# A modulation stage written anew: reversed rows from the input, the norm in the weights, the bias in PSUM

## The chip, the cores and the metric

The program runs on one core of one Trainium2 chip. The metric is the device time of one launch in microseconds (us). Engines are named as in the profile: PE (TensorE, with its weight loads as PEld), DVE (VectorE), ACT (ScalarE), POOL (GpSimd) and SP, which issues most transfers. A line such as L1242 is a line of the kernel before, if nothing else is said.

## The reference

The program computes a text/vision block and a quantised feed-forward over 4096 rows of 512 channels. Attention (not touched) leaves, for each row, a vector `u` of 384 numbers, and `c_t @ W_film_in` is computed as `u` times weights folded beforehand. What the change touches is the input modulation, which stands in front of a convolution along the rows:

```python
def _layernorm(x, axis=-1, eps=1e-05):
    m = jnp.mean(x, axis=axis, keepdims=True)
    v = jnp.var(x, axis=axis, keepdims=True)
    return (x - m) / jnp.sqrt(v + eps)
...
x = layernorm(x_text, g_norm_in, b_norm_in)      # x_text is itself _layernorm(x)
scale_in, shift_in = jnp.split(c_t @ W_film_in + b_film_in, 2, axis=-1)
x = x * (1.0 + mod_gate * scale_in) + mod_gate * shift_in
y = s4d(x, log_dt, A_re, A_im, C_re, C_im, D_skip)
```

## The kernel before

The program is a row of phases with a barrier between each two: `prepare`, `attention`, `modulate`, `s4d`, `feed_forward`, `bit_feed_forward`. Each engine has its own written-out instruction stream, in a fixed order, and waits on semaphores. Only `modulate` is changed (and the host's layout of one input).

`modulate` handles 32 tiles of 128 rows, with the two buffers of each name used in turn, tile n in buffer n % 2. `prepare` has left the normalised input in `scratch_xt` and the folded weights in `scratch_wf_in` (384 x 1024: 512 columns for the scale and 512 for the shift), `attention` has left `scratch_u` (4096 x 384). For each tile:

- SP loads `mod_xt` (L1187, when DVE has read that buffer, `xt_read`) and `mod_u` (L1189, when PE has turned it).
- PE turns `u` by three transposes into `mod_tp` (L1319). ACT rounds it into the high part of `mod_uT` (L1277), DVE subtracts for the low part (L1236).
- PE multiplies (L1329): high x high, high x low, low x high, three chunks each, 9 matmuls of 512 columns for the scale and 9 for the shift, into `mod_film`.
- DVE takes the mean and variance of `xt` (L1226, L1228), ACT the root (L1273), DVE the reciprocal (L1230) and the normalised tile `mod_xn` (L1232). POOL multiplies by the gain (L1201) and adds the offset (L1203).
- DVE adds the film bias to both halves (L1242, L1243), multiplies by `xn` (L1246) and adds the shift (L1249) into `mod_xm`.
- `s4d` wants the rows of each tile in reversed order. ACT rounds `xm` into a high part (L1284), POOL subtracts for the low part (L1207), PE multiplies both with a matrix of ones on the other diagonal (L1338, L1339) into `mod_rev`, and ACT copies that into `X` (L1290), where successive channels lie 32 numbers (128 bytes) apart.

Before the loop, the weights are loaded whole and split into high and low parts by DVE (L1254, L1256). In the loop, one turn of DVE is `normalise(n + 1)` then `film(n)`; one turn of PE is `turn_u(n + 2)`, `film(n + 1)`, `reverse(n)`; one turn of ACT is `root(n + 2)`, `copy_u(n + 2)`, `high_x(n)`, `copy_x(n)`.

Of the kernel before, what the change touches and what calls it, by code (L numbers as in the profile page):

```python
# [1145 lines left out]
def modulate(nc, sem, const, a, W, root_table, wf, fb, X, dram):  # L1146

# [3 lines left out]
    with scope:  # L1151
# [15 lines left out]
        rstd = sb("mod_rstd", [P, 1])
        tp = [ps(f"mod_tp{k}", [P, VC, P]) for k in range(2)]
        fp = [ps(f"mod_film{k}", [P, 2, BANK]) for k in range(2)]
        rp = [ps(f"mod_rev{k}", [P, BANK]) for k in range(2)]  # L1170
        x_by_channel = X[:].rearrange("p c d -> p (c d)").rearrange("p (d c) -> p d c", c=TILES)
        s = {n: sem("mod_" + n) for n in (
            "wf_loaded", "tables_in", "rows_in", "in0", "in1", "xt_read", "u_turned", "uT_ready", "film_done", "film_read", "std_wanted", "std_ready",
            "normed", "affine", "diag_made", "wf_split", "uT_high", "xm_ready", "xm_high", "xm_split", "reversed", "X_ready", "passed")}

        with nc.Block() as block:
            @block.sync
            def _(sp):
                sp.dma_start(wf[:], dram["wf_in"][:, :, :]).then_inc(s["wf_loaded"], 16)
                sp.dma_start(fb[:], dram["fb"][1, :].partition_broadcast(P)).then_inc(s["rows_in"], 16)  # L1180
                sp.dma_start(gain[:], a["g_norm_in"].partition_broadcast(P)).then_inc(s["rows_in"], 16)
                sp.dma_start(offset[:], a["b_norm_in"].partition_broadcast(P)).then_inc(s["rows_in"], 16)
                with sp.Fori(0, TILES // 2) as i:
                    for b in range(2):
                        n = 2 * i + b
                        sp.wait_ge(s["xt_read"], n + 1)
                        sp.dma_start(xt[:, b], dram["xt"][bass.ts(n, P), :]).then_inc(s[f"in{b}"], 16)  # L1187
                        sp.wait_ge(s["u_turned"], n + 1)
                        sp.dma_start(u[:, b], dram["u"][bass.ts(n, P), :]).then_inc(s[f"in{b}"], 16)  # L1189

            @block.gpsimd
            def _(pool):
                nc.gpsimd.memset(other_diag[:], 0.0)
                pool.drain()
                nc.gpsimd.affine_select(out=other_diag[:], in_=other_diag[:], compare_op=ALU.not_equal, fill=1.0,
                                        base=1 - P, pattern=[[1, P]], channel_multiplier=1).then_inc(s["diag_made"], 1)
                pool.wait_ge(s["rows_in"], 48)

                def affine(m, b):
                    pool.wait_ge(s["normed"], 2 * m + b + 1)  # L1200
                    nc.gpsimd.tensor_tensor(xn[:, b], xn[:, b], gain[:], ALU.mult)  # L1201
                    pool.drain()
                    nc.gpsimd.tensor_tensor(xn[:, b], xn[:, b], offset[:], ALU.add).then_inc(s["affine"], 1)  # L1203

                def low_x(m, b):
                    pool.wait_ge(s["xm_high"], 2 * m + b + 1)
                    nc.gpsimd.tensor_tensor(xm_parts[:, b, 1], xm[:, b], xm_parts[:, b, 0].bitcast(F32), ALU.subtract).then_inc(s["xm_split"], 1)  # L1207

                pool.sem_inc(s["xm_split"], 2)
                affine(0, 0)  # L1210
                with pool.Fori(0, TILES // 2 - 1) as i:
                    for b in range(2):
                        affine(*after(i, b))
                        low_x(i, b)
                affine(TILES // 2 - 1, 1)
                low_x(TILES // 2 - 1, 0)
                low_x(TILES // 2 - 1, 1)

            @block.vector
            def _(dve):  # L1220
                dve.sem_inc(s["xt_read"], 2)

                def normalise(m, b):
                    n = 2 * m + b
                    dve.wait_ge(s[f"in{b}"], 32 * (m + 1))
                    nc.vector.bn_stats(stats[:], xt[:, b, :])  # L1226
                    dve.drain()
                    nc.vector.bn_aggr(mv[:], stats[:]).then_inc(s["std_wanted"], 1)  # L1228
                    dve.wait_ge(s["std_ready"], n + 1)
                    nc.vector.reciprocal(rstd[:], rstd[:])  # L1230
                    dve.drain()
                    nc.vector.tensor_scalar(xn[:, b], xt[:, b], mv[:, 0:1], rstd[:, 0:1], ALU.subtract, ALU.mult).then_inc(s["normed"], 1)  # L1232
                    dve.drain()
                    dve.sem_inc(s["xt_read"], 1)
                    dve.wait_ge(s["uT_high"], n + 1)
                    nc.vector.tensor_tensor(uT[:, b, 1], tp[b][:], uT[:, b, 0].bitcast(F32), ALU.subtract).then_inc(s["uT_ready"], 1)  # L1236

                def film(m, b):
# [24 lines left out]
                normalise(TILES // 2 - 1, 1)
# [1658 lines left out]
```

## Time and profile before

| what | us |
|---|---|
| median of 3 runs | 4269.23 (4267.5 to 4271.36) |
| the profiled execution, its time | 4266.21 |
| the profiled execution, its span | 4264.4 |
| of that: modulation, from its first transfer's issue (1963.38) to the end of its last copy into X (2206.45 + 1.02) | 244.1 |

Over the span PE is busy 78%, DVE 76%, ACT 54% and POOL 33%, at a mean granted TensorE clock of 0.834. Phases stand behind one another with a barrier, so a phase's length goes whole into the time, and an engine's share over the span tells nothing of this phase. The views that follow are of the stretch from 1963 to 2208 us.

### The profile page before, as it was taken

To read this page: it belongs to the slowest core of one execution; us is meant where nothing else is said; L and a number is where in the kernel's file an instruction comes from. 1 tells how busy PE (TensorE), PEld (TensorE's weight loads), DVE (VectorE), ACT (ScalarE), POOL (GpSimd) and SP (SyncE) were. 2 spreads that over 40 slices of the span, in tenths; PEclk is the share of its full clock that TensorE was granted. 3 is DMA by queue.
4 is the path that set the end of the run, shared out by engine and by line. 5 is a ranking of instruction groups with operands and counts; after the bars stand their busy time and mean duration, and the time that the engine had idled before them with its cause. 6 is when DMAs were issued, how large, how long until landed. Compare 5 with 4: busy or idle time off the path is not lost. (4 is left out here: it accounts for less than half of the span.)

```text
span 4264.4 us, 55224 instructions
## 1 busy us (share of the span) xinstructions
PE 3337.1 (78%) x16624; PEld 2225.8 (52%) x16624; DVE 3241.3 (76%) x8831; ACT 2284.6 (54%) x3031; POOL 1425.2 (33%) x1265
## 2 busy tenths in 40 slices
PE   7665858888888888876757778568999999936776
PEld 3343535555555555544545555357777777712333
DVE  7699999999999999986889999334443434369996
ACT  4574858887778888882323333223332332337774
POOL 0022424444444444443551010023233323205664
PEclk9756767777777777778978998889999999968888
DMA  8600000000000000002212343444433333330111
GB/s 321 242 6 9 10 5 9 9 9 12 9 11 9 9 9 9 9 7 90 67 33 52 88 104 86 119 138 144 124 129 123 126 116 92 121 92 26 54 49 53
DMA packets 263808, 291.04 MB, mean 68 GB/s; under 512 B 55450, under 2 KB 177436, under 8 KB 262368
## 3 DMA queue, kind: packets, MB, share of 16 engines
q1 hardware_dynamic: 240504, 255.10, 19.6%
q10 hardware_dynamic: 19976, 17.80, 1.5%
q0 software_dynamic: 3040, 14.94, 0.9%
q8 instruction: 102, 1.67, 0.2%
q14 instruction: 186, 1.52, 0.1%
HBM read 219.34 MB, written 68.45 MB: 67 GB/s over the span
## 5 line engine op out<-in xcount | busy, mean ns | idle before, releaser
L1061 PE MATMUL score<-KT,q 64*128 64x512 f32 (+1 forms) x1792 | 669.9, 522 | 276.5 <-ACT S L918 159.8
L815 DVE MAX8 cand<-S 128x8 f32<-128x100 f32 (+1 forms) x4096 | 680.4, 245 | 69.9 <-ACT S L918 50.2
L1061 PEld LDWEIGHTS score<-KT,q 64*128 64x128 f32 x1792 | 439.6, 264 | 509.5 <-ACT S L918 219.6
L1089 PE MATMUL up<-ctx,attnT 128*128 128x384 f32 (+1 forms) x1664 | 614.1, 518 | 0.0
L918 ACT ACTIVATE S<-score 128x1024 f32<-128x1024 f32 (+1 forms) x512 | 406.6, 832 | 107.3 <-PE score L1061 107.3
L820 DVE SCALAR_TENSOR_TENSOR S<-S,tops,E 128x3202 f32<-128x3202 f32 x128 | 449.4, 3553 | 10.6 <-ACT E L949 10.6
L1089 PEld LDWEIGHTS up<-ctx,attnT 128*128 128x128 f32 (+1 forms) x1664 | 324.3, 205 | 210.4 <-issue 55.5
L2150 DVE TENSOR_TENSOR ff_gelu<-ff_whole,ff_gelu 128x512 fp32r<-128x512 f32 x128 | 98.3, 768 | 429.5 <-ACT ff_gelu L2277 429.5
L927 ACT ACTIVATE E<-S,below 128x3202 bf16<-128x3202 f32 x128 | 379.7, 2966 | 26.1 <-issue 11.7
L949 ACT ACTIVATE E<-S,ebias 128x3202 f32<-128x3202 f32 x128 | 379.7, 2967 | 1.0 <-DVE S L820 0.7
L2386 PE MATMUL ff_acc<-ff_W,ff_gelu 128*128 128x512 f32 x1024 | 344.4, 397 | 0.0
L780 POOL TENSOR_TENSOR S<-S 128x512 f32<-128x512 f32 (+1 forms) x217 | 243.5, 1159 | 295.2 <-DVE S L820 295.2
L773 POOL TENSOR_TENSOR S<-S 128x512 f32<-128x512 f32 (+1 forms) x224 | 223.3, 1033 | 340.4 <-DVE S L820 340.4
L2276 ACT ACTIVATE ff_whole<-ff_fp,ff_b 128x512 f32<-128x512 f32 x128 | 88.0, 687 | 396.7 <-PE ff_fp L2371 396.5
L2371 PE MATMUL ff_fp<-ff_hT,ff_W 128*128 128x512 f32 x1024 | 265.8, 402 | 3.5 <-ACT ff_gelu L2277 2.1
L2748 PE MATMUL bf_hp<-bf_qin,bf_W1q 128*128 128x458 bf16 (+1 forms) x576 | 158.8, 430 | 119.0 <-DVE bf_conv L2589 100.7
L1079 PE MATMUL turn<-ident,S 128*128 128x128 f32 x832 | 174.3, 352 | 91.7 <-ACT attnT L958 70.0
L2543 POOL TENSOR_TENSOR bf_silu<-bf_silu,bf_scale 128x912 f32<-128x912 f32 (+1 forms) x67 | 161.8, 2451 | 212.8 <-ACT bf_scale L2700 212.8
L2386 PEld LDWEIGHTS ff_acc<-ff_W,ff_gelu 128*128 128x128 f32 x1024 | 192.8, 188 | 45.5
L2371 PEld LDWEIGHTS ff_fp<-ff_hT,ff_W 128*128 128x128 f32 x1024 | 189.7, 189 | 46.6 <-ACT ff_gelu L2277 2.5
L784 POOL TENSOR_TENSOR S<-S 128x512 f32<-128x512 f32 (+1 forms) x217 | 208.0, 993 | 4.9 <-issue 4.9
L844 DVE MAX8 tops<-cand 128x8 f32<-128x256 f32 x512 | 193.1, 419 | 19.7
(359 smaller groups left out, 6278.0 us busy)
## 6 DMA issues: line engine op xcount, KB each, us to landing
s_hankel<-scratch_K SPq DMA_DIRECT2D x128, 256.0 KB, 4.5
ff_w_low<-scratch_w1l SPq DMA_DIRECT2D x112, 256.0 KB, 2.6
ff_w_low<-scratch_w2l SPq DMA_DIRECT2D x112, 256.0 KB, 2.7
xt_prep<-in_x SPq DMA_DIRECT2D x8, 1024.0 KB, 8.6
scratch_xt<-xt_prep SPq DMA_DIRECT2D x8, 1024.0 KB, 8.3
next_prep<-in_ffn_w_t POOLq DMA_DIRECT2D x8, 1024.0 KB, 11.3
q<-scratch_qt SPq DMA_DIRECT2D x128, 64.0 KB, 1.9
mod_xt<-scratch_xt SPq DMA_DIRECT2D x32, 256.0 KB, 2.7
```

Of the source, the lines that this page charges most:

```text
L773: nc.gpsimd.tensor_tensor(S[:, b, 0, chunk(j)], S[:, b, 0, chunk(j)], S[:, b, 1, chunk(j)], ALU.add).then_inc(s["summed01"], 1)
L780: nc.gpsimd.tensor_tensor(S[:, b, 0, chunk(j)], S[:, b, 0, chunk(j)], S[:, b, 2, chunk(j)], ALU.add).then_inc(s["summed02"], 1)
L784: nc.gpsimd.tensor_tensor(S[:, b, 0, chunk(j)], S[:, b, 0, chunk(j)], S[:, b, 3, chunk(j)], ALU.add).then_inc(s["summed"], 1)
L815: nc.vector.max(cand[:, h, 8 * k:8 * k + 8], S[:, b, h, k * SEG:end])
L820: nc.vector.scalar_tensor_tensor(S[:, b, h, :], S[:, b, h, :], tops[:, b, h, TOP - 1:TOP], E[:, h % 2, :], ALU.is_ge, ALU.mult).then_inc(s ...
L918: nc.scalar.activation(S[:, b, h, 2 * BANK * k:2 * BANK * k + w], score[k % 2][:, :, :].rearrange("p c k -> p (c k)")[:, 0:w], ACT.Copy).t ...
L927: nc.scalar.activation(signs, S[:, b, h, :], ACT.Sign, bias=below[:, h:h + 1], accum_out=count[:, h:h + 1]).then_inc(s["counted"], 1)
L949: nc.scalar.activation(E[:, h % 2, :], S[:, b, h, :], ACT.Exp, bias=ebias[:, b, h:h + 1], scale=SCALE).then_inc(s["e_ready"], 1)
L1061: last = nc.tensor.matmul(score[k % 2][:, j % 2, 0:w], lhsT=q[at, part, h // 2, :], rhs=KT[at, h // 2, chunk(j)], start=(part == 0), stop= ...
L1089: last = nc.tensor.matmul(up[:, 0:DV], lhsT=attnT[0:w, e, c - 4 * g, :], rhs=ctx[0:w, c, :], start=(c == 0), stop=(c == GC - 1))
L2371: last = nc.tensor.matmul(fp[f % 2][:], lhsT=left, rhs=hT[:, h_part, c, :], start=(j == 0), stop=(j == len(terms) - 1))
L2386: last = nc.tensor.matmul(acc[:, k, :], lhsT=gelu[:, g_part, F % RING, k * P:(k + 1) * P], rhs=right, start=(f == 0 and j == 0), stop=(f = ...
```

## The change

The input is laid out a second time by the host, as `x_turned`, with the 128 rows of each tile reversed. The modulation reads that instead of `scratch_xt`; since this is the raw input, the two norms are taken in one (variance times 1 + eps, plus eps squared, under the root). The transposed `u` is read with its columns reversed, so that the film's rows come out reversed too. The reversal by matmul, its two splits and the copy into `X` are gone.

The gain and the offset of the norm are multiplied into the weights ahead of the loop (`wg`, `wb`), by DVE, and the high parts of both are rounded by ACT. The film's bias (also scaled, by POOL on two rows) is added in PSUM by a matmul of 512 columns over two rows, one for each half. For each tile, DVE then does two fused steps: (x - mean) * scale part into `mod_part`, and that times the reciprocal root plus the shift part, straight into `X`. SP's loop is written out, ACT issues the loads of gain, offset and bias, and `u` is loaded ahead of `x`.

```diff
 SP
+                def load(m, b):
+                    n = 2 * m + b
+                    sp.wait_ge(s["u_turned"], n + 1)
+                    sp.dma_start(u[:, b], dram["u"][n * P:(n + 1) * P, :]).then_inc(s[f"uin{b}"], 16)
+                    sp.wait_ge(s["x_read"], n + 1)
+                    sp.dma_start(xt[:, b], a["x_turned"][n * P:(n + 1) * P, :]).then_inc(s[f"xin{b}"], 16)
+                sp.dma_start(wf[:, :, 0:D], dram["wf_in"][:, :, 0:D]).then_inc(s["ws_in"], 16)
+                load(0, 0)
+                sp.dma_start(wf[:, :, D:2 * D], dram["wf_in"][:, :, D:2 * D]).then_inc(s["wh_in"], 16)
+                load(0, 1)
+                for n in range(2, TILES):
+                    load(n // 2, n % 2)
 DVE
+                def stats_of(m, b):
+                    dve.wait_ge(s[f"xin{b}"], 16 * (m + 1))
+                    nc.vector.bn_stats(stats[:, b], xt[:, b, :])
+                    dve.drain()
+                    nc.vector.bn_aggr(mv[:, b], stats[:, b]).then_inc(s["std_wanted"], 1)
+                def low_u(m, b):
+                    dve.wait_ge(s["uT_high"], 2 * m + b + 1)
+                    nc.vector.tensor_tensor(uT[:, b, 1], tp[b][:, :, ::-1], uT[:, b, 0].bitcast(F32), ALU.subtract).then_inc(s["uT_ready"], 1)
                 def film(m, b):
-                    dve.drain()
-                    dve.wait_ge(s["film_done"], n + 1)
-                    nc.vector.tensor_tensor(sc[:], fp[b][:, 0, :], fb[:, 0:D], ALU.add)
-                    nc.vector.tensor_tensor(sh[:, b], fp[b][:, 1, :], fb[:, D:2 * D], ALU.add).then_inc(s["film_read"], 1)
-                    dve.drain()
-                    dve.wait_ge(s["affine"], n + 1)
-                    nc.vector.tensor_tensor(sc[:], xn[:, b], sc[:], ALU.mult)
-                    dve.drain()
-                    dve.wait_ge(s["xm_split"], n + 1)
-                    nc.vector.tensor_tensor(xm[:, b], sc[:], sh[:, b], ALU.add).then_inc(s["xm_ready"], 1)
+                    dve.wait_ge(s["std_ready"], n + 1)
+                    nc.vector.reciprocal(rstd[:, b:b + 1], rstd[:, b:b + 1])
+                    dve.wait_ge(s["film_done"], 2 * n + 1)
+                    nc.vector.scalar_tensor_tensor(part[:, b], xt[:, b], mv[:, b, 0:1], fp[b][:, 0, :], ALU.subtract, ALU.mult).then_inc(s["x_read"], 1)
+                    dve.drain()
+                    dve.wait_ge(s["film_done"], 2 * n + 2)
+                    nc.vector.scalar_tensor_tensor(x_by_channel[:, :, bass.ds(n, 1)], part[:, b].unsqueeze(2), rstd[:, b:b + 1], fp[b][:, 1, :].unsqueeze(2),
+                                                   ALU.mult, ALU.add).then_inc(s["film_read"], 1)
...
+                nc.vector.tensor_tensor(wg[:], wf[:, :, 0:D], gain[:].unsqueeze(1).broadcast_to(every), ALU.mult).then_inc(s["wg_ready"], 1)
+                nc.vector.tensor_tensor(wb[:], wf[:, :, 0:D], offset[:].unsqueeze(1).broadcast_to(every), ALU.mult)
+                dve.wait_ge(s["wg_high"], 1)
+                nc.vector.tensor_tensor(wf_parts[:, 1, :, 0:D], wg[:], wf_parts[:, 0, :, 0:D].bitcast(F32), ALU.subtract).then_inc(s["w_split"], 1)
...
+                nc.vector.tensor_tensor(wb[:], wb[:], wf[:, :, D:2 * D], ALU.add).then_inc(s["wh_ready"], 1)
+                low_u(0, 0)
...
+                nc.vector.scalar_tensor_tensor(fb_parts[:], fb_high[:].bitcast(F32), is_low[:, 0:1], fbg[:], ALU.mult, ALU.subtract).then_inc(s["fb_ready"], 1)
+                dve.wait_ge(s["wh_high"], 1)
+                nc.vector.tensor_tensor(wf_parts[:, 1, :, D:2 * D], wb[:], wf_parts[:, 0, :, D:2 * D].bitcast(F32), ALU.subtract).then_inc(s["w_split"], 1)
 ACT
+                    nc.scalar.activation(rstd[:, b:b + 1], mv[:, b, 1:2], ACT.Sqrt, bias=eps2[:, 0:1], scale=1.0 + EPS).then_inc(s["std_ready"], 1)
+                    nc.scalar.activation(uT[:, b, 0], tp[b][:, :, ::-1], ACT.Copy).then_inc(s["uT_high"], 1)
 PE
+                        for k, (x, w) in enumerate(((0, 0), (0, 1), (1, 0))):
+                            for c in range(VC):
+                                nc.tensor.matmul(fp[b][:, half, :], lhsT=uT[:, b, x, c, :], rhs=wf_parts[:, w, c, at], start=(k == 0 and c == 0), stop=False)
+                        nc.tensor.matmul(fp[b][:, half, :], lhsT=minus_r[:], rhs=fb_parts[:, at], start=False, stop=True).then_inc(s["film_done"], 1)
```

On DVE, one tile of the loop of the modulation stood so before:

```order
L1226 BN_STATS mod_stats<-mod_xt 128x6
L1228 BN_AGGR mod_mv<-mod_stats 128x2
L1229 ISA
L1230 RECIPROCAL mod_rstd<-mod_rstd 128x1
L1232 TENSOR_SCALAR mod_xn<-mod_xt,mod_mv,mod_rstd 128x512
L1236 TENSOR_TENSOR mod_uT<-mod_tp,mod_uT 128x384
L1242 TENSOR_TENSOR mod_scale<-mod_film,fb_in 128x512
L1243 TENSOR_TENSOR mod_shift<-mod_film,fb_in 128x512
L1246 TENSOR_TENSOR mod_scale<-mod_xn,mod_scale 128x512
L1249 TENSOR_TENSOR mod_xm<-mod_scale,mod_shift 128x512
```

And with the change (lines of the changed kernel; the fused steps are L1229 and L1232):

```order
L1216 BN_STATS mod_stats<-mod_xt 128x6
L1218 BN_AGGR mod_mv<-mod_stats 128x2
L1221 ISA
L1222 TENSOR_TENSOR mod_uT<-mod_tp,mod_uT 128x384
L1227 RECIPROCAL mod_rstd<-mod_rstd 128x1
L1228 ISA
L1229 SCALAR_TENSOR_TENSOR mod_part<-mod_xt,mod_mv,mod_film 128x512
L1231 REGISTER_ALU
L1232 ISA
L1232 SCALAR_TENSOR_TENSOR X<-mod_part,mod_rstd,mod_film 128x512
```

Six passes over 512 elements have become three; the first three rows of compute are of tile n + 1 and the last three of tile n, and `mod_xt` of tile n, last read ahead of `mod_uT` of tile n before, is now read once more at L1229, behind the statistics of tile n + 1.

On PE, one tile of the loop before (in the second, the changed kernel's):

```order
L1319 MATMUL mod_tp<-ident,mod_u 128x128 x3
L1324 ISA
L1329 MATMUL mod_film<-mod_wf,mod_uT 128x512 x18
L1336 REGISTER_ALU
L1338 MATMUL mod_rev<-mod_xm_parts,mod_anti 128x512
L1339 MATMUL mod_rev<-mod_xm_parts,mod_anti 128x512
```

```order
L1305 MATMUL mod_tp<-ident,mod_u 128x128 x3
L1310 ISA
L1318 MATMUL mod_film<-mod_wf_parts,mod_uT 128x512 x9
L1321 MATMUL mod_film<-mod_fb_parts,mod_minus_r 128x512
L1318 MATMUL mod_film<-mod_wf_parts,mod_uT 128x512 x9
L1321 MATMUL mod_film<-mod_fb_parts,mod_minus_r 128x512
```

The two matmuls of the reversal have gone from the end of a tile, and two of the bias have come, one behind each half; there are 20 of 512 columns in both.

On ACT, one tile of the loop before and with the change:

```order
L1273 ACTIVATE mod_rstd<-mod_mv,eps 128x1
L1276 REGISTER_ALU
L1277 ACTIVATE mod_uT<-mod_tp 128x384
L1281 REGISTER_ALU
L1284 ACTIVATE mod_xm_parts<-mod_xm 128x512
L1288 REGISTER_ALU
L1290 ISA
L1290 ACTIVATE X<-mod_rev 128x512
```

```order
L1274 ACTIVATE mod_rstd<-mod_mv,mod_eps 128x1
L1277 REGISTER_ALU
L1278 ACTIVATE mod_uT<-mod_tp 128x384
```

The copy of `u` still stands behind the root of the same tile, and that is now the whole turn.

## Rows read from the trace of the kernel before

**Rows 1.** Windows: us, busy (count) per engine, granted clock, DMA share, GB/s.

```profile
core 0: us, PE busy (x) PEld busy (x) DVE busy (x) ACT busy (x) POOL busy (x), PEclk, DMA share, GB/s
1989.70:2196.00 206.30, 161.52 (x675) 122.61 (x674) 175.04 (x265) 68.04 (x118) 119.00 (x89) 0.95 0.19 62
2007.00:2014.00 7.00, 6.87 (x25) 5.17 (x24) 5.46 (x10) 2.43 (x5) 4.14 (x4) 0.76 0.18 66
2063.00:2070.00 7.00, 5.33 (x26) 4.07 (x25) 6.02 (x10) 2.34 (x4) 4.14 (x4) 1.00 0.23 82
```

**Rows 2.** Timeline of one tile in the loop: start us, duration us, engine, line.

```profile
start us, us, engine line op out<-in xcount [idle before <-releaser]
2095.57 0.56 DVE L1236 TENSOR_TENSOR mod_uT<-mod_tp,mod_uT 128x384 fp32r<-128x384 f32 x1
2095.65 0.33 SPq L1187 DMA_DIRECT2D mod_xt<-scratch_xt  x1
2096.29 0.69 DVE L1242 TENSOR_TENSOR mod_scale<-mod_film,fb_in 128x512 f32<-128x512 f32 x1 [0.16 <-issue]
...
2096.90 0.68 DVE L1243 TENSOR_TENSOR mod_shift<-mod_film,fb_in 128x512 f32<-128x512 f32 x1
...
2097.48 0.49 PE L1319 MATMUL mod_tp<-ident,mod_u 128*128 128x128 f32 x3
2097.67 0.97 DVE L1246 TENSOR_TENSOR mod_scale<-mod_xn,mod_scale 128x512 f32<-128x512 f32 x1
2097.70 3.97 PEld L1329 LDWEIGHTS mod_film<-mod_wf,mod_uT 128*128 128x128 f32 x18
2097.73 4.37 PE L1329 MATMUL mod_film<-mod_wf,mod_uT 128*128 128x512 f32 x18
...
2098.24 1.56 POOL L1203 TENSOR_TENSOR mod_xn<-mod_xn,mod_offset 128x512 f32<-128x512 f32 x1
2098.72 1.63 DVE L1249 TENSOR_TENSOR mod_xm<-mod_scale,mod_shift 128x512 f32<-128x512 f32 x1
2100.27 0.68 DVE L1226 BATCH_NORM_STATS2 mod_stats<-mod_xt 128x6 f32<-128x512 f32 x1
2101.02 0.18 DVE L1228 BATCH_NORM_AGGREGATE mod_mv<-mod_stats 128x2 f32<-128x6 f32 x1
2101.24 0.29 ACT L1273 ACTIVATE mod_rstd<-mod_mv,eps 128x1 f32<-128x1 f32 x1 [2.25 <-DVE mod_mv L1228]
2101.44 0.47 ACT L1277 ACTIVATE mod_uT<-mod_tp 128x384 fp32r<-128x384 f32 x1
2101.57 0.16 DVE L1230 RECIPROCAL mod_rstd<-mod_rstd 128x1 f32<-128x1 f32 x1 [0.36 <-ACT mod_rstd L1273]
2101.81 0.55 DVE L1232 TENSOR_SCALAR mod_xn<-mod_xt,mod_mv,mod_rstd 128x512 f32<-128x512 f32 x1
...
2102.49 0.56 DVE L1236 TENSOR_TENSOR mod_uT<-mod_tp,mod_uT 128x384 fp32r<-128x384 f32 x1
...
2102.58 0.33 SPq L1187 DMA_DIRECT2D mod_xt<-scratch_xt  x1
```

**Rows 3.** From the tile view of mod_xt, 2000 to 2180 us: its loads.

```profile
DMA to landing us min/median/max: 2.4/2.6/2.8
```

**Rows 4.** Tile view of mod_wf, the film's matmuls: duration ns min/median/max.

```profile
L1329 PE MATMUL mod_film<-mod_wf,mod_uT x576: 387/389/794, 1979.2 to 2199.8; 128*128 128x512 f32 x192
```

**Rows 5.** Groups by form: a strided and a dense output on ACT; a fused DVE step.

```profile
L1290 ACT ACTIVATE X<-mod_rev 128x512 f32 x30 | 34.0, 1133 | 71.6 <-PE mod_rev L1339 71.6
L1284 ACT ACTIVATE mod_xm_parts<-mod_xm 128x512 fp32r<-128x512 f32 x32 | 19.8, 620 | 1.7 <-DVE mod_xm L1249 1.7
L2631 DVE SCALAR_TENSOR_TENSOR bf_x<-bf_op,bf_undo,bf_x 114x512 f32<-114x512 f32 x32 | 23.7, 743 | 7.4 <-PE bf_op L2784 7.4
```

**Rows 6.** Timeline of the start of the modulation.

```profile
1963.38 0.35 SPq L1179 DMA_DIRECT2D wf_in<-scratch_wf_in  x1
...
1969.64 1.76 DVE L1254 CAST mod_wf<-wf_in 128x3072 fp32r<-128x3072 f32 x1 [5.29 <-DMA wf_in<-scratch_wf_in]
1971.48 3.36 DVE L1256 TENSOR_TENSOR mod_wf<-wf_in,mod_wf 128x3072 fp32r<-128x3072 f32 x1
...
1976.02 1.28 ACT L1273 ACT_TABLE_LOAD   x1 [15.58 <-DVE mod_mv L1228]
...
1979.17 6.19 PE L1329 MATMUL mod_film<-mod_wf,mod_uT 128*128 128x512 f32 x18 [2.19 <-DVE mod_uT L1236]
...
1986.79 0.69 DVE L1246 TENSOR_TENSOR mod_scale<-mod_xn,mod_scale 128x512 f32<-128x512 f32 x1
1987.55 0.69 DVE L1249 TENSOR_TENSOR mod_xm<-mod_scale,mod_shift 128x512 f32<-128x512 f32 x1
```

**Rows 7.** Timeline of the end of the modulation and the next phase's first instruction.

```profile
2206.45 1.02 ACT L1290 ACTIVATE X<-mod_rev 128x512 f32<-128x512 f32 x1 [2.74 <-PE mod_rev L1339]
2208.46 0.11 POOL L1468 MEMSET s_skip<- 128x16 f32 x1 [3.41 <-POOLq L2811]
```

More of the change, by code:

```diff
@@ L1143, in _, with modulate @@
                 turn(TILES + 1, 1, old=False, new=False, newer=False, last=True)
[L1146 removed]
+def modulate(nc, sem, const, a, W, root_table, X, dram):
     scope, sb, ps = phase_scope(nc)
@@ L1194, in _ @@
+                nc.gpsimd.memset(minus[:], -1.0)
+                nc.gpsimd.memset(is_low[:], 1.0)
                 pool.drain()
[L1195 to L1214, printed above, removed]
@@ L1215, in _ @@
-                affine(TILES // 2 - 1, 1)
-                low_x(TILES // 2 - 1, 0)
-                low_x(TILES // 2 - 1, 1)
+                nc.gpsimd.memset(is_low[0:1], 0.0).then_inc(s["signs_made"], 1)
+                pool.wait_ge(s["norm_in"], 32)
+                pool.wait_ge(s["fb_in"], 16)
+                nc.gpsimd.tensor_tensor(fbg[:, D:2 * D], fb[:, 0:D], offset[0:2], ALU.mult)
+                nc.gpsimd.tensor_tensor(fbg[:, 0:D], fb[:, 0:D], gain[0:2], ALU.mult)
+                pool.drain()
@@ L1267, in _ @@
             @block.scalar
             def _(act):
-                act.sem_inc(s["X_ready"], 2)
+                act.dma_start(gain[:], a["g_norm_in"].partition_broadcast(P)).then_inc(s["norm_in"], 16)
+                act.dma_start(offset[:], a["b_norm_in"].partition_broadcast(P)).then_inc(s["norm_in"], 16)
+                act.dma_start(fb[:], dram["fb"][1, :].partition_broadcast(2)).then_inc(s["fb_in"], 16)
                 def root(m, b):
                     act.wait_ge(s["std_wanted"], 2 * m + b + 1)
-                    nc.scalar.activation(rstd[:], mv[:, 1:2], ACT.Sqrt, bias=const["eps"][:, 0:1]).then_inc(s["std_ready"], 1)
@@ L1298, in _ @@
-                copy_u(0, 1)
+                root(0, 0)
                 with act.Fori(0, TILES // 2 - 1) as i:
                     for b in range(2):
-                        root(i + 1, b)
-                        copy_u(i + 1, b)
-                        high_x(i, b)
-                        copy_x(i, b)
-                for b in range(2):
-                    high_x(TILES // 2 - 1, b)
-                    copy_x(TILES // 2 - 1, b)
-                act.wait_ge(s["X_ready"], TILES + 2)
+                        root(*after(i, b))
+                        high_u(*after(i, b))
@@ L1309, in _ @@
+                root(TILES // 2 - 1, 1)
+                high_u(TILES // 2 - 1, 1)
                 act.wait_ge(s["tables_in"], 32)
@@ L1320, in turn_u, with film @@
                     last.then_inc(s["u_turned"], 1)
-                def film(m, b):
+                def film(m, b, first=False):
                     n = 2 * m + b
```

145 lines of the change are left out of this document (54 added, 91 removed).

## The prediction

> **What bounds the kernel now.** Phases stand behind barriers, so I looked only at the stretch of the modulation: 244.1 us from its first transfer to its last copy [rows 6, 7]. The windows come first [rows 1]: in the loop, from 1989.7 to 2196.0, DVE is busy 175.0 of 206.3 us (85%), PE 161.5 (78%), POOL 119.0, ACT 68.0, and the transfers take 19%. No engine is full, so next I read the timeline of one tile [rows 2]. The reader should take the distance between two instances of L1236 there: 2095.57 to 2102.49, 6.92 us for a tile, and the issues of L1187 agree (2095.65 to 2102.58, 6.93). 32 tiles at that pace are 221 us, nearly the whole stage. In that distance DVE is busy 0.56 + 0.69 + 0.68 + 0.97 + 1.63 + 0.68 + 0.18 + 0.16 + 0.55 = 6.10 us, and its only longer wait is that for the root, 0.36. So DVE's chain sets the pace, and PE has slack: its tile is 4.37 for the film and some 0.9 for transposes and reversal. Two of DVE's steps are longer than they need be: L1246 and L1249 take 0.97 and 1.63 while POOL works on its own tiles, and 0.69 each in the one tile where POOL is idle [rows 2, 6].
>
> **What the change takes from each engine.** POOL has nothing left in the loop. ACT keeps the root (0.29) and the copy of u (0.47). PE trades two reversal matmuls for two bias matmuls of as many columns. The 18 film matmuls start within 3.97 us, 0.2206 each; 20 are 4.41, and with the transposes (2097.48 to 2097.73, 0.25) PE's own pace would be 4.7 us a tile, 4.8 with hand-overs. DVE keeps statistics (0.68 + 0.18), reciprocal (0.16) and low u (0.56), loses L1232, L1242, L1243, L1246 and L1249, and gains two fused steps. The nearest row for the first fused step is L2631, a fused step of 512 elements with one operand in PSUM: 0.743 us [rows 5]. The second one writes X with 128 bytes between elements. No DVE row does that. Its lower bound is the same 0.74. For the upper one I take ACT's strided copy, 1.133, against its dense one, 0.620: 0.51 more, so 1.25; I use 1.25, since it is the same output with the same stride, and double that surcharge (1.8) as the end. DVE's work is then 0.68 + 0.18 + 0.56 + 0.16 + 0.74 + 1.25 = 3.6 us a tile, against 6.1.
>
> The Trainium skill (SBUF — State Buffer, section "SBUF: two separate sides") says that each access that moves on to a new 16-byte line costs extra; the ACT rows agree, and by it the second fused step is above 0.74 too.
>
> If work alone set the pace, PE at 4.8 would be the bound. It is not, and this is the step on which my number rests.
>
> **Who is late next: the load of x.** Before, a tile's x was last read by L1232, in the half turn before its film; its buffer was refilled two tiles ahead. Now x of tile n is read a second time by the first fused step, in `film(n)`. Only then may SP load x of tile n + 2 into that buffer, and the very next thing DVE does behind the second fused step of tile n is the statistics of tile n + 2. So the load has one tile's time, not two, and it lies in a ring that comes round once a tile: fused step 1 of tile n, load, statistics, root, copy of u, low u, reciprocal, fused step 1 of tile n + 1. The copy of u does not need the root, but stands behind it on ACT, so it is in the ring. What is queued behind DVE's wait for x is low u and so PE's next film. Step by step:
>
> - end of the first fused step to SP's issue: L1232 ends at 2102.36 and L1187 issues at 2102.58, 0.22 with a drain between that now falls away: 0.2 [rows 2].
> - issue to landing: 2.6, between 2.4 and 2.8 [rows 3]. It is the same size from another tensor.
> - landing to bn_stats: no row of the loop shows this, because x is never late before. Other hand-overs there take 0.04 to 0.2; I take 0.1.
> - bn_stats start to bn_aggr start: 0.75; to the root's start: 0.22; to the copy's start: 0.20; the copy: 0.47; to DVE: 0.04, as from the end of L1273 to L1230 [rows 2].
> - low u, 0.56 less the overlap with the next instruction (L1242 starts 0.61 before L1243 and takes 0.69): 0.5. Reciprocal to the first fused step: 0.24 with a drain before, now without: 0.2.
> - the fused step: 0.74 [rows 5].
>
> Sum: 0.2 + 2.6 + 0.1 + 0.75 + 0.22 + 0.20 + 0.47 + 0.04 + 0.5 + 0.2 + 0.74 = **6.0 us a tile**. With the load at 2.4, hand-overs at zero where I guessed (0.3 less) it is 5.5; with 2.8, and 0.1 more at two hand-overs with registers, 6.4. The second fused step (1.25, or 1.8) lies beside the load of 2.8 in all and costs nothing here: that is its cover, and without it 0.5 us would come on a tile. PE's 4.8 is below 6.0 and leaves 1.2 idle.
>
> **The start.** The wait for weights was 6.3 us (1963.38 to 1969.64, the whole 1536 KB) [rows 6]. The first half is asked for alone, but wg also needs gain and offset, behind each other on ACT's queue; I take 5.5. Then DVE has 1536 elements per instruction; L1256 had 3072 in 3.36, so 1.7 each. Five of them (wg, wb, two splits, one sum) are 8.5, with low u 0.56, the bias rows (0.2, 0.6, 1.2) and drains, 11.3: up to 16.8 us from the start. The statistics of tile 0 are 0.9, the ACT table load 1.28 and root 0.29, then root and copy for tile 1, 0.7, low u and reciprocal 0.7, first fused step 0.74: it ends at 21.4. PE's first film starts behind low u (some 12.5 against 15.8 before), and is no later than that even at its slow pace of 0.34 a matmul (6.19 for 18) [rows 6]. **The end.** After the first fused step of tile 30 the last film still has to run: low u of tile 31 ended 0.95 earlier, 20 matmuls are 4.6, and the last fused step 1.25 with hand-over 0.2: 5.1 on.
>
> **The sum.** 21.4 + 30 x 6.0 + 5.1 = 206.5, against 244.1: **37.6 us less**. The barrier behind it costs the same, 0.99 [rows 7]. The profiled execution took 4266.2, so 4228.6; the median of the runs is 3.0 above it, which gives **4231**. The bounds of the ring (5.5 and 6.4) make it 4216 and 4243; the start and the end may be off by 3 us either way, together 4213 to 4246.
>
> **Dips of the clock.** In most of the loop the granted clock is 1.00, but it was 0.76 from 2007 to 2014, one of six such stretches that make the 0.95 of the whole loop [rows 1]. PE was then busy 6.87 of 7.00, where 5.33 is usual, so a dip costs PE 1.5 us and was just covered. With 1.2 us of slack, 0.3 would be left over for a dip; for six or ten dips that is 2 or 3 us, inside the range.
>
> **The rivals.**
> *PE sets the pace.* If the ring were much shorter than its rows say (the load landing in under 1.5 us would do), a tile would cost 4.8: 31 x 1.2 = 37 less again, 4194. For it: PE and DVE do have that little work. Against: the load took 2.4 at least in 26 of 26 cases. 7%.
> *Reversed reads are dear.* ACT and DVE now read the transposed u backwards. No row before has a backward read. From below: nothing. From above: as dear as ACT's stride, 1.133 / 0.620 = 1.8 times: 0.39 and 0.46 more, both in the ring: 6.85 a tile, 26 us back, 4257. Half of that gives 4244. A neighbour is still a neighbour backwards, so I hold it at 12%, spread between 4244 and 4257.
> *The clock stays low: slower than before.* PE has pauses of 1.2 us behind every film. The film's matmuls take 387 ns at the full clock of 2.4 GHz and up to 794 at 1.2 [rows 4]; at the lower level throughout, PE's tile would be about 2 x 4.7 = 9.4 us, and the stage 22 + 31 x 9.4 + 8 = 321, 77 us longer than before: 4346. It becomes slower than before when PE's tile passes 7.2 us, a mean granted clock near 0.65. For it: dips are there already, and the clock was 0.76 in such a stretch. Against: before, PE was busy 78% of the loop with pauses as long, and the mean was 0.95; with 4.7 to 5.2 of 6.0 it will be at least as busy. 5%. The Trainium skill (TensorE: Matmul & The Clock Gate, section "A second HAM failure mode: psum-queue depth-cycling") describes a kernel whose short pauses between groups of matmuls made the clock swing; by that rule the same could be here, and the dips of the rows agree that it can.
> *The change gives nothing* (within 8.5 us): a ring of 7.0 to 7.5, which needs dear reversed reads and a slower second fused step (over 3.3) at once. 3%.
>
> **How the numbers follow.** Forecast, a ring of 5.5 to 6.4: 73%, 4213 to 4246. I widen the range to take in most of the reversed reads and a ring somewhat shorter: 4205 to 4256. Outside are PE's pace, the low clock and the no-gain case, some 17%. A measurement of this kernel can tell 0.2%, 8.5 us, from no change. Faster by more: forecast, PE's pace and reversed reads, 92%. Within: 3%. Slower: 5%.
>
> **What would show it.** In the profile after: DVE's bn_stats idle before it, released by the DMA of mod_xt, some 1.5 us a tile; the loads of mod_xt issued once in 6.0 us; bn_stats and low u 1.7 apart; the first fused step 0.74 and the second 1.25; the ring wrong if PE's film waits for nothing, or if bn_stats never waits for a DMA. POOL empty in the loop. The stage from its first issue to the last write of X: 206 us. I would be wrong by the largest sum if the step that I have from no row (the landing's hand-over, the reversed reads, the strided write beyond 2.8) is not small.

## The result, and the profile after

The changed kernel takes **4229.4 us** in the median of four runs (4225.1 to 4231.1), the kernel before beside it 4269.5 (4267.5 to 4271.4): a ratio of 0.9906, with a 95% interval of 0.9890 to 0.9921. The prediction was 4231 in 4205 to 4256, and "faster by over 0.2%". Sign, size and range hold. The inside of the number holds less well: its three terms, the start, the loop and the end, were off by +4, -10 and +3 us, and most of that cancelled.

The profiled execution has a span of 4227.0 us against 4264.4, 37.4 less. Its modulation runs from 1963.59 to 2167.05, 203.5 us against 244.1, 40.6 less; the phase behind it starts 40.5 us earlier. The missing 3 us went in the phases behind, the same code in both kernels: from the first instruction of the next phase to the end of the span they take 2055.9 us before and 2059.0 after, and in the ten profiles of the experiments below between 2052.6 and 2058.9. So I take the 3 us for scatter of those phases. The 4229 so owes some of its closeness to 4231 to luck: the stage came out 3 us shorter than predicted and the rest of the span 3 us longer.

The timeline of one tile in the loop after (start us, duration us; the answer to [rows 2]):

```profile
2091.16 0.73 DVE L1229 SCALAR_TENSOR_TENSOR mod_part<-mod_xt,mod_mv,mod_film 128x512 f32<-128x512 f32 x1
2091.92 0.33 SPq L1187 DMA_DIRECT2D mod_xt<-in_x_turned  x1
2092.21 0.18 PEld L1321 LDWEIGHTS mod_film<-mod_fb_parts,mod_minus_r 2*128 2x128 f32 x1 [0.35 <-issue]
2092.21 0.50 PE L1321 MATMUL mod_film<-mod_fb_parts,mod_minus_r 2*128 2x512 f32 x1
...
2092.64 0.55 PE L1305 MATMUL mod_tp<-ident,mod_u 128*128 128x128 f32 x3
2092.84 1.16 DVE L1232 SCALAR_TENSOR_TENSOR X<-mod_part,mod_rstd,mod_film 128x512 f32 x1 [0.95 <-PE mod_film L1321]
...
2092.94 2.30 PE L1318 MATMUL mod_film<-mod_wf_parts,mod_uT 128*128 128x512 f32 x9
2094.33 0.70 DVE L1216 BATCH_NORM_STATS2 mod_stats<-mod_xt 128x6 f32<-128x512 f32 x1 [0.32 <-DMA mod_xt<-in_x_turned]
...
2095.17 0.50 PE L1321 MATMUL mod_film<-mod_fb_parts,mod_minus_r 2*128 2x512 f32 x1
...
2095.60 2.34 PE L1318 MATMUL mod_film<-mod_wf_parts,mod_uT 128*128 128x512 f32 x9
2096.02 0.56 DVE L1222 TENSOR_TENSOR mod_uT<-mod_tp,mod_uT 128x384 fp32r<-128x384 f32 x1 [0.74 <-ACT mod_uT L1278]
2096.49 0.15 DVE L1227 RECIPROCAL mod_rstd<-mod_rstd 128x1 f32<-128x1 f32 x1
2096.56 0.73 DVE L1229 SCALAR_TENSOR_TENSOR mod_part<-mod_xt,mod_mv,mod_film 128x512 f32<-128x512 f32 x1
```

Two things are to be seen. DVE waits, as predicted, for the load of x (0.32 in front of bn_stats), but it also waits 0.95 for PE in front of the second fused step. And PE, from 2092.94 on, never waits for another engine: it goes from one group to the next, 5.66 us for a tile, though its matmuls need 20 x 0.2206. Over the 30 tiles from the first fused step at 1988.52 to that of tile 30 at 2158.73 the pace is 5.67 us. ("Pace" is this distance between the first fused steps of two tiles. With two buffers for x it is given as the mean of these 30 tiles, with four buffers, where it is steadier, as the value in the middle of the loop.)

Who waited for whom from 2000 to 2140 us (us in all, times, longest):

```profile
DVE X L1232 <- PE mod_film L1321: 33.1, 25, 1.7
DVE mod_stats L1216 <- DMA mod_xt<-in_x_turned: 6.0, 12, 0.7
```

DVE waits for PE in all 25 tiles, and for the load of x in only 12, 0.25 us a tile in all where the prediction looked for 1.5. PE's film waits for nothing, and that was one of the prediction's signs that the ring is wrong. The experiments settle what this sign is worth.

Two windows of the loop after, in the columns of [rows 1]:

```profile
core 0: us, PE busy (x) PEld busy (x) DVE busy (x) ACT busy (x) POOL busy (x), PEclk, DMA share, GB/s
2008.00:2014.00 6.00, 6.00 (x27) 4.22 (x27) 3.47 (x7) 0.67 (x2) 0.00 (x0) 1.00 0.31 112
2092.00:2098.00 6.00, 6.00 (x26) 4.01 (x24) 3.31 (x6) 0.67 (x2) 0.00 (x0) 1.00 0.22 76
```

PE shows as busy all the time, POOL has left, DVE is at 55 to 60%, and the granted clock is 1.00. It is 0.99 or 1.00 in every window of six microseconds from 1990 to 2164; the dips of [rows 1] are gone.

The groups of the changed instructions (mean ns after the comma; the answer to [rows 5]):

```profile
L1232 DVE SCALAR_TENSOR_TENSOR X<-mod_part,mod_rstd,mod_film 128x512 f32 x30 | 35.0, 1166 | 40.5 <-PE mod_film L1321 40.5
L1229 DVE SCALAR_TENSOR_TENSOR mod_part<-mod_xt,mod_mv,mod_film 128x512 f32<-128x512 f32 x32 | 23.3, 729 | 1.5 <-PE mod_film L1321 1.5
L1216 DVE BATCH_NORM_STATS2 mod_stats<-mod_xt 128x6 f32<-128x512 f32 x32 | 22.1, 691 | 7.2 <-DMA mod_xt<-in_x_turned 6.8
L1222 DVE TENSOR_TENSOR mod_uT<-mod_tp,mod_uT 128x384 fp32r<-128x384 f32 x32 | 17.8, 557 | 22.9 <-ACT mod_uT L1278 22.9
L1278 ACT ACTIVATE mod_uT<-mod_tp 128x384 fp32r<-128x384 f32 x32 | 15.1, 471 | 0.0
```

The first fused step takes 0.729 (predicted 0.74), the strided one 1.166 (1.25). The two that now read PSUM backwards take 0.557 and 0.471, what their forward forms took [rows 2]: the backward read costs nothing.

And the start (the answer to [rows 6]):

```profile
1963.59 0.60 SPq L1189 DMA_DIRECT2D mod_wf<-scratch_wf_in  x1
...
1971.67 2.13 DVE L1238 TENSOR_TENSOR mod_wg<-mod_wf,mod_gain 128x1536 f32<-128x1536 f32 x1 [31.23 <-DMA mod_wf<-scratch_wf_in]
...
1972.15 2.77 POOL L1206 TENSOR_TENSOR mod_fbg<-mod_fb,mod_gain 2x512 f32<-2x512 f32 x1
...
1973.73 2.81 DVE L1239 TENSOR_TENSOR mod_wb<-mod_wf,mod_offset 128x1536 f32<-128x1536 f32 x1
...
1975.06 2.59 POOL L1208 TENSOR_TENSOR mod_fbg<-mod_fbg,mod_fb 2x512 f32<-2x512 f32 x1
...
1976.46 2.81 DVE L1241 TENSOR_TENSOR mod_wf_parts<-mod_wg,mod_wf_parts 128x1536 fp32r<-128x1536 f32 x1
1979.37 1.76 DVE L1244 TENSOR_TENSOR mod_wb<-mod_wb,mod_wf 128x1536 f32<-128x1536 f32 x1
```

Here lies the surprise of the start: DVE can begin 8.1 us after the first issue, not 5.5, and three of DVE's instructions take 2.1 to 2.8 us for what the fourth does in 1.76, while POOL works on two rows. Gain and offset were not the late ones: they landed 4.0 and 6.9 us after their issue. The half of the weights came last, in 8.1 us, where the whole took 6.3 before. Gain and offset now load beside it from ACT's queue, and the other half, `u` and `x` are issued behind it before it lands; no run takes them apart, so why the half came so late stays open.

### The profile page after: what moved, and what is told of

Read it like the earlier page. It is cut to its first block and busy times, and to the rows that moved or that the text cites. A ratio compares the mean times of both kernels' runs of the same rounds, so it can differ in the third digit from the quotient of the medians.

```text
span 4227.0 us, 54424 instructions
## 1 busy us (share of the span) xinstructions
PE 3342.4 (79%) x16624; PEld 2217.5 (52%) x16624; DVE 3165.3 (75%) x8740; ACT 2234.5 (53%) x2969; POOL 1300.7 (31%) x1174
```

## The experiments

The question after the result: which of two limits sets the 5.67, PE's own tile (theory A) or the ring through the load of x (theory B, the prediction's)? All ratios are to the kernel before, run beside each.

**Without the bias matmuls.** The stop and the semaphore move to the last film matmul of each half.

```diff
...
-                        nc.tensor.matmul(fp[b][:, half, :], lhsT=minus_r[:], rhs=fb_parts[:, at], start=False, stop=True).then_inc(s["film_done"], 1)
+                        last.then_inc(s["film_done"], 1)
...
```

> The changed kernel without the two bias matmuls of a tile (the film's bias is left out). Theory A: PE sets the changed kernel's pace of 5.67 us a tile, since each two-row bias matmul costs it about 0.7 us and not 0.22; then PE's own tile falls to 4.7, the ring through the load of x takes over at about 5.4, and the time falls by 30 x 0.27, 8 us, to 4221. Theory B: the ring through the load of x already sets the pace; then no change, 4229, and PE idles 0.9 us a tile.

Measured: 4224.0 us, ratio 0.9905 (0.9888 to 0.9921), the same as the changed kernel's; pace 5.65. Two lines of who waited for whom, 2000 to 2130 us (us in all, times, longest):

```profile
DVE mod_stats L1216 <- DMA mod_xt<-in_x_turned: 28.8, 23, 1.4
PE mod_film L1318 <- DVE mod_uT L1222: 21.3, 23, 1.1
```

These are theory B's numbers: no change, PE idle 0.9 us a tile, DVE waiting for the load in every tile, 1.25 us each. The ring is a limit at 5.65. But that does not clear PE.

**Four buffers for x.** The x of a tile stands in buffer n % 4, DVE's loop is written over four tiles, and x is loaded two tiles earlier.

```diff
-        xt = sb("mod_xt", [P, 2, D])
+        xt = sb("mod_xt", [P, 4, D])
...
```

> The changed kernel with four buffers for x instead of two, and nothing else. Theory A (PE's tile of 5.66 sets the pace): the time stays at 4229, and bn_stats no longer waits for a transfer. Theory B (the ring through the load of x sets it): the pace falls to about 4.8 us a tile, 27 us less, 4202.

Measured: 4224.9 us, ratio 0.9908 (0.9891 to 0.9924); pace 5.66, in the middle of the loop 5.64 to 5.66 tile after tile. The waits now hold no line for mod_xt; what DVE waits for is PE:

```profile
DVE X L1234 <- PE mod_film L1327: 39.6, 23, 1.7
```

That is theory A's number. Each limit stands at 5.65 or 5.66 when the other is away.

**Both.** Four buffers and no bias matmuls, the two edits above together.

> Both: four buffers for x and no bias matmuls (the film's bias is left out). Under either theory neither limit is left and PE's 18 film matmuls and three transposes set the pace: 18 x 0.2206 + 0.3 = 4.3 us a tile, or 4.7 if hand-overs come on top; 4229 - 30 x (5.67 - 4.7) = 4200, down to 4188 at 4.3. If it is no faster than without bias alone, the ring was never a limit, if no faster than four buffers alone, PE was none.

Measured: 4184.7 us, ratio 0.9813 (0.9797 to 0.9830); pace 4.44, within the expected 4.3 to 4.7; the time is 3 us under the expected 4188. Each edit alone gave nothing that can be told, both together 40 us. So the changed kernel has two limits of equal length, and each experiment with one edit alone would have led to a wrong conclusion. The prediction's ring is one of the two, although PE's film never waits in the changed kernel. PE's own tile without bias is 18 x 0.2206 plus 0.48 for the transposes' turn.

**Bias over 128 rows, four buffers.** The two rows stay; 126 rows of zeros are added to both operands.

```diff
...
-        fb_parts = sb("mod_fb_parts", [2, 2 * D], F32R)
+        fb_parts = sb("mod_fb_parts", [P, 2 * D], F32R)
...
-        minus_r = sb("mod_minus_r", [2, P], F32R)
+        minus_r = sb("mod_minus_r", [P, P], F32R)
...
```

> The changed kernel with four buffers for x and with the bias matmuls over 128 rows (two of them as before, 126 zero). It computes all. If the dear part of the bias matmul is that it has two rows (its weight load does not overlap the matmul in front of it), it now costs 0.22 us like any other: 20 x 0.2206 + 0.3 = 4.7 us a tile, 4229 - 30 x 0.95 = 4201. If the price is that of a matmul at the end of each half, whatever its rows, nothing is gained: 4229.

Measured: **4198.2 us**, ratio 0.9843 (0.9827 to 0.9860), computing everything; pace 4.93. Its PE from one half to the next, beside the same place with two rows above:

```profile
2083.78 0.19 PEld L1332 LDWEIGHTS mod_film<-mod_fb_parts,mod_minus_r 128*128 128x128 f32 x1
...
2084.02 0.39 PE L1332 MATMUL mod_film<-mod_fb_parts,mod_minus_r 128*128 128x512 f32 x1
2084.02 2.01 PEld L1329 LDWEIGHTS mod_film<-mod_wf_parts,mod_uT 128*128 128x128 f32 x9
...
2084.25 2.22 PE L1329 MATMUL mod_film<-mod_wf_parts,mod_uT 128*128 128x512 f32 x9
```

With 128 rows the weight load starts 0.24 ahead of its matmul, and the next matmul follows 0.23 after. With two rows, in the timeline after, the load starts with its own matmul (2092.21 both), behind an idle stretch of 0.35, and the next group follows 0.43 after. The two bias matmuls cost 0.49 us a tile over 128 rows (4.93 - 4.44) and 1.22 over two (5.66 - 4.44). Here two rows are dearer than 128; no other number of rows was run, and why the weight load of two rows does not start early is not shown.

**Bias over 128 rows, two buffers.** The same edit without the extra buffers.

> The changed kernel with the bias matmuls over 128 rows, and still two buffers for x. If the changed kernel has two limits that happen to be equal, PE's tile with two-row bias matmuls (5.66) and the ring through the load of x (5.65), this takes away the first alone: pace 5.65, time within 4 us of the changed kernel's, PE idle some 0.7 us a tile. If PE's tile were the only limit it would be 4.9 a tile, 23 us less.

Measured: 4219.5 us, ratio 0.9892 (0.9876 to 0.9909); pace 5.62 and the wait for mod_xt 28.5 us in 23 tiles. The pace is the ring's. The time is some 6 us below the changed kernel's ratio, where the intervals still overlap, and a little more than I expected; in the profiles the next phase starts 3.4 us earlier (2164.7 against 2168.1), 4.1 counted from each one's first issue, since PE's last two films are shorter and no longer behind.

**Bias matmuls side by side, two rows, four buffers.**

```diff
...
+                    if not first:
+                        for half in range(2):
+                            nc.tensor.matmul(fp[b][:, half, :], lhsT=minus_r[:], rhs=fb_parts[:, half * D:(half + 1) * D], start=True, stop=False)
...
```

> Four buffers for x; the two two-row bias matmuls of a tile stand side by side ahead of its 18 film matmuls (but for the first tile). If the price is paid at each change between 128 rows and 2 rows, half of it goes: 5.66 - 0.5 = 5.2 us a tile, some 14 us less than with four buffers alone. If each two-row matmul pays by itself, nothing goes: 5.66.

Measured: 4214.4 us, ratio 0.9878 (0.9862 to 0.9895); pace 5.32 against 5.66. So 0.34 went and not the 0.5 expected, but the 0.5 was too much: two matmuls over two rows cost 1.22 - 0.49 = 0.73 more than over 128, and half of that is 0.37. With half of the changes between 128 rows and two gone, nearly half of the surcharge went. So most of it belongs to the change and not to each matmul. The two stand as one piece in the trace, with the idle time at the entry and at the exit:

```profile
2085.49 0.29 PEld L1320 LDWEIGHTS mod_film<-mod_fb_parts,mod_minus_r 2*128 2x128 f32 x2 [0.17 <-issue]
2085.49 0.73 PE L1320 MATMUL mod_film<-mod_fb_parts,mod_minus_r 2*128 2x512 f32 x2
...
2086.15 3.97 PEld L1325 LDWEIGHTS mod_film<-mod_wf_parts,mod_uT 128*128 128x128 f32 x18 [0.37 <-issue]
```

**The copy of u ahead of the root.** Now the ring's own sum is tested, by taking the root and the copy out of it, on two buffers.

```diff
-                        root(*after(i, b))
                         high_u(*after(i, b))
+                        root(*after(i, b))
```

With 128 rows of bias:

> Bias matmuls over 128 rows, two buffers for x, and on ACT the copy of u ahead of the root of the same tile instead of behind it. It computes all. If the ring through the load of x is made of the steps as added up in the prediction, the root's hand-over, root and copy (0.21 + 0.20 + 0.47 + 0.03) leave it but for the hand-over to low u: 5.65 - 0.85 = 4.8, and PE's own 4.9 becomes the limit: 4.9 us a tile, 22 us less than the changed kernel, with no further memory. If the ring is another, the pace stays at 5.65.

Measured: **4199.2 us**, ratio 0.9842 (0.9825 to 0.9858), computing everything; pace 4.90. DVE now waits for the load in 12 of 27 tiles and for PE in all, so PE is the limit again. One reordered line is worth as much as two more buffers. And without bias, so that PE is out of the way:

> Two buffers for x, no bias matmuls (the film's bias is left out), the copy of u ahead of the root on ACT. PE's own tile is 4.45 here, so the ring is bare: with the root and the copy out of it, 5.65 - 0.85 = 4.8 us a tile, 26 us less than without bias alone, 4198. If the whole of the gain in the kernel with 128 rows and this order came from the bias matmuls, the pace stays at 5.65.

Measured: 4201.2 us, ratio 0.9850 (0.9833 to 0.9866); pace 4.81, against 5.65 without the swap: 0.84 shorter where the four steps add up to 0.91, and 0.85 when some hand-over to low u is left. DVE waits for the load in each of 27 tiles, 1.2 us each. So root and copy are in the ring, as the prediction has them, and four buffers have shown that the load is. Its other steps were read off the timeline, not taken out one by one.

**The kernel before, without POOL's gain and offset.** This asks where the 40 us come from.

```diff
-                    nc.gpsimd.tensor_tensor(xn[:, b], xn[:, b], gain[:], ALU.mult)
-                    pool.drain()
-                    nc.gpsimd.tensor_tensor(xn[:, b], xn[:, b], offset[:], ALU.add).then_inc(s["affine"], 1)
+                    pool.sem_inc(s["affine"], 1)
...
```

> The kernel before, with POOL's multiplication by the gain and addition of the offset left out (the tile passes unchanged); everything else stays. If DVE's chain sets the pace of 6.92 and L1246 and L1249 are long only because POOL works beside them, they fall from 1.0 and 1.62 to 0.69 each and the pace to 5.7 us: 31 x 1.2, 37 us less than before, as much as the whole change gave. If DVE's instructions are long for another reason or another chain sets the pace, the time stays within 10 us of before.

Measured: 4233.7 us, ratio 0.9921 (0.9905 to 0.9938), 33 us less than before; the expectation had 37. The pace is 5.82 where 5.7 was expected: every second tile is some 0.3 longer, with DVE waiting for PE's film and PE for POOL's low part of `xm`. The two DVE steps, unchanged in the code, without POOL's gain and offset and then in the kernel before:

```profile
L1247 DVE TENSOR_TENSOR mod_xm<-mod_scale,mod_shift 128x512 f32<-128x512 f32 x32 | 22.2, 693 | 2.4
L1244 DVE TENSOR_TENSOR mod_scale<-mod_xn,mod_scale 128x512 f32<-128x512 f32 x32 | 22.2, 693 | 3.0
```

```profile
L1249 DVE TENSOR_TENSOR mod_xm<-mod_scale,mod_shift 128x512 f32<-128x512 f32 x32 | 45.5, 1421 | 2.4
L1246 DVE TENSOR_TENSOR mod_scale<-mod_xn,mod_scale 128x512 f32<-128x512 f32 x32 | 35.7, 1115 | 2.9
L1242 DVE TENSOR_TENSOR mod_scale<-mod_film,fb_in 128x512 f32<-128x512 f32 x32 | 22.1, 692 | 12.0 <-PE mod_film L1329 9.2 <-issue 1.3
```

The means fall from 1421 and 1115 ns to 693. L1242, of the same size, also runs beside POOL in the kernel before (2096.29 to 2096.98, POOL's L1207 and L1201 beside it) and is not lengthened: 691 to 693 ns in all 32 tiles, and in the first of them POOL is idle. It has one operand in PSUM, L1246 and L1249 have both in SBUF. So most of what the whole change gave was to be had by taking POOL out of the way of those two; what DVE's lost passes could have given beyond that was cut off by the two limits at 5.65.

**The bias rows scaled by DVE instead of POOL**, on the kernel with 128 rows and four buffers. All three instructions of the scaling move; the first is shown.

```diff
...
-                nc.gpsimd.tensor_tensor(fbg[:, D:2 * D], fb[:, 0:D], offset[0:2], ALU.mult)
+                nc.vector.tensor_tensor(fbg[:, D:2 * D], fb[:, 0:D], offset[0:2], ALU.mult)
...
```

> Four buffers for x, bias matmuls over 128 rows, and the scaling of the bias rows ahead of the loop done by DVE instead of POOL. It computes all. Against the same kernel with POOL's scaling (4198, ratio 0.9843): if DVE's three instructions on the weights took 2.13, 2.81 and 2.81 us and not 1.7 because POOL's three ran beside them, they fall to 1.75 each and the first film starts 2.6 us earlier; DVE then has 2.1 us of scaling to do itself while PE works on the first half. Net 1 to 3 us less, 4196, at the edge of what can be told. If the long instructions had another cause, 2 us more, 4200.

Measured: 4199.3 us, ratio 0.9840 (0.9824 to 0.9857), no difference that can be told. The long instructions did fall:

```profile
1971.43 1.76 DVE L1239 TENSOR_TENSOR mod_wg<-mod_wf,mod_gain 128x1536 f32<-128x1536 f32 x1 [6.62 <-DMA mod_wf<-scratch_wf_in]
...
1973.11 1.75 DVE L1240 TENSOR_TENSOR mod_wb<-mod_wf,mod_offset 128x1536 f32<-128x1536 f32 x1
...
1974.80 1.76 DVE L1242 TENSOR_TENSOR mod_wf_parts<-mod_wg,mod_wf_parts 128x1536 fp32r<-128x1536 f32 x1
...
1978.94 4.21 PE L1328 MATMUL mod_film<-mod_wf_parts,mod_uT 128*128 128x512 f32 x9 [2.98 <-DVE mod_uT L1220]
```

The first film starts 15.5 us after the first issue; in the changed kernel it was 18.1. But DVE's three instructions for the rows, and its waiting, fill the time up to the first fused step, which starts 24.8 us after the first issue with either engine. The start's end is set by DVE's chain, not by PE's first film.

## Why the prediction was right, and where it was not

**What bounded the kernel before: right.** DVE's chain with POOL beside it; the run without POOL's gain and offset shows it, with the 0.69 that the prediction read off the one undisturbed tile. The pace of 6.92 was that of an undisturbed tile too: with the dips of the clock five tiles of 8.4 are each followed by one of 6.0, 14.4 for two where 13.8 is usual, and the mean of 30 tiles is 6.99. So the dips were not quite covered and cost some 2 us.

**Who is late next: right in kind, but not alone.** The x of a tile is read again one step later and its reload comes into a ring of one tile. In the kernel without bias matmuls the ring stands bare:

```profile
2083.89 0.73 DVE L1229 SCALAR_TENSOR_TENSOR mod_part<-mod_xt,mod_mv,mod_film 128x512 f32<-128x512 f32 x1
...
2084.65 0.33 SPq L1187 DMA_DIRECT2D mod_xt<-in_x_turned  x1
...
2087.28 0.69 DVE L1216 BATCH_NORM_STATS2 mod_stats<-mod_xt 128x6 f32<-128x512 f32 x1 [1.23 <-DMA mod_xt<-in_x_turned]
...
2088.05 0.18 DVE L1218 BATCH_NORM_AGGREGATE mod_mv<-mod_stats 128x2 f32<-128x6 f32 x1
...
2088.26 0.29 ACT L1274 ACTIVATE mod_rstd<-mod_mv,mod_eps 128x1 f32<-128x1 f32 x1 [4.95 <-DVE mod_mv L1218]
2088.46 0.47 ACT L1278 ACTIVATE mod_uT<-mod_tp 128x384 fp32r<-128x384 f32 x1
2088.97 0.56 DVE L1222 TENSOR_TENSOR mod_uT<-mod_tp,mod_uT 128x384 fp32r<-128x384 f32 x1 [0.74 <-ACT mod_uT L1278]
2089.44 0.15 DVE L1227 RECIPROCAL mod_rstd<-mod_rstd 128x1 f32<-128x1 f32 x1
2089.51 0.73 DVE L1229 SCALAR_TENSOR_TENSOR mod_part<-mod_xt,mod_mv,mod_film 128x512 f32<-128x512 f32 x1
```

Its terms beside the prediction's:

| step | predicted | measured |
|---|---|---|
| fused step's end to issue | 0.2 | 0.03 |
| issue to bn_stats | 2.7 | 2.63 |
| bn_stats to bn_aggr, to root, to copy | 0.75, 0.22, 0.20 | 0.77, 0.21, 0.20 |
| copy, and to low u | 0.51 | 0.50 |
| low u to reciprocal, to the fused step | 0.5, 0.2 | 0.47, 0.07 |
| fused step | 0.74 | 0.73 |
| sum | 6.0 | 5.6 |

What was mis-sized are the hand-overs that had a drain or a register in them before: 0.2 each taken, 0.03 and 0.07 measured. The expected wait of 1.5 us for the load stands only where PE is out of the way (1.25 without bias matmuls); in the changed kernel it is 0.25. The pace term, 30 x 6.0, came out as 30 x 5.67, 10 us less.

**PE's pace of 4.8: wrong.** The step that failed is "20 are 4.41": it gave a two-row matmul the distance of a 128-row one. That nearly holds for 128 rows (4.93 measured against 4.8), not for two (5.66). The prediction named no bound for it, although the change adds a form that no row of the loop shows. By luck the missed 0.86 brought PE's tile to the length of the ring, so it cost nothing that shows in the time; but the prediction's "leaves 1.2 idle" is false, and so was the rival at 4194: with the ring gone, four buffers alone stay at 4225.

**The second fused step.** 1.25 predicted by ACT's stride surcharge, 1.166 measured; the surcharge on DVE is 0.44 over the dense fused step, against ACT's 0.51. Its cover, the load, holds it: in the timeline after, it ends at 2094.00 and bn_stats starts at 2094.33. The Trainium skill (SBUF — State Buffer, "SBUF: two separate sides") says that an access that moves on to a new 16-byte line costs extra; with 128 bytes between elements each write does so, and this row agrees with it for a write by DVE.

**Start and end.** Predicted 21.4, measured 25.7 (1963.59 to 1989.27): the half of the weights landed 2.6 later than I took. DVE's work ahead of the first statistics took 13.6 instead of 11.3, with three instructions that took 7.8 beside POOL's three on two rows where I had 1.7 each. Behind it 4.0 was left instead of 4.6: the ACT table load of 1.28, which I had in the chain, ran beside DVE's work on the bias rows, and the statistics of tile 1, which I did not have, filled part of its place. I had seen POOL's effect on DVE in the loop and not looked for it in the start. The end took 7.6 instead of 5.1: the last film started 1.7 us after its low u was ready, since PE was still at tile 30 (2160.48 against 2158.75), and takes 5.4 with its two-row bias where I had 4.6. 25.7 + 170.2 + 7.6 = 203.5. (The prediction's 4228.6 + 3.0 is 4231.6, which it gives as 4231; nothing hangs on it.)

**The rivals.** Backward reads: free (0.557 and 0.471 against 0.56 and 0.47). The low clock: the opposite came, the dips went, with PE never idle for another engine. That PE's steady work is what removed them is not shown: in the kernel before without POOL's gain and offset PE still waits for POOL, 0.6 us a tile and up to 0.9, and the granted clock is 1.00 in every window of seven microseconds from 1993 to 2168. The run without bias matmuls has pauses of 0.9 us in every tile, and there the granted clock was still 1.00 from 1995 to 2140; pauses of that size did not bring it down here. The Trainium skill (TensorE: Matmul & The Clock Gate, "A second HAM failure mode: psum-queue depth-cycling") tells of a kernel in which short pauses between groups of matmuls made the clock swing; no run of the change shows that, and the changed kernel has no such pauses.

## What to carry to other kernels

When a step reads a buffer again later in the turn, draw the ring of what frees it, what reloads it and what waits for the load, and add that ring up as carefully as any engine's work: here one line that shortened it gave 21 us with full bias matmuls (0.9892 to 0.9842), half as much as the whole change. When two limits lie close together, an experiment on one of them shows nothing; take both away, then each alone. And before counting a new instruction at the price of its neighbours, look whether its shape is theirs: padding two rows to 128 made the matmul cheaper, and one line moved on ACT gave, with it, 27 us more (0.9842 against 0.9906 of 4267).

## What the runs showed of the hardware

- A matmul over two rows between matmuls over 128 costs more than one over 128: in a tile with two of them 5.66 us against 4.93. The weight load does not start ahead of its matmul (0.35 idle before it, 0.25 before the next; 0.17 and 0.37 where two stand side by side).
- A POOL instruction on two partitions (2x512) slows a DVE instruction on 128 with both operands in SBUF, as a wide one does: 2.81 us against 1.76 for 1536 elements, and 1.42 or 1.12 against 0.69 for 512 beside POOL on 128 partitions. POOL's own on two rows take 2.6 to 2.8 beside DVE, and 1.25 the one that ran mostly ahead of it. A DVE instruction with one operand in PSUM was not slowed (L1242 of the kernel before, 691 to 693 ns with POOL beside it and without).
- Reading PSUM backwards along the row costs neither ACT nor DVE anything (0.471 and 0.557 us for 384 elements, against 0.472 and 0.558 forwards).
- DVE's write with 128 bytes between elements costs 1.166 us for 512 elements, against 0.729 dense.
